# Two attention rows spread by TensorE, the stages around the first and last batch in another order, and elu added to x in two VectorE passes

## The reference, cut to what matters

```python
x: (8, 1024, 128) f32;  adj: (8, 1024, 1024) int32, 0 or 1, about 1 in 64 set
def gat(h, adj, W, a):                      # a graph attention layer
    Wh = h @ W
    e = (Wh @ a1)[:, :, None] + (Wh @ a2)[:, None, :]
    e = where(e > 0, e, 0.2 * e)            # leaky relu
    p = softmax(where(adj > 0, e, -big), axis=-1)
    return p @ Wh
x = x + elu(gat(relu(layernorm(x)), adj, W0, a0))     # layer 0
x = x + gat(relu(layernorm(x)), adj, W1, a1)          # layer 1
```

## Time and profile before

| what | value |
|---|---|
| median of 3 runs | 315.14 us (313.93 to 317.64) |
| the profiled execution, device time | 314.74 us |
| its span | 312.9 us |
| TensorE matmul busy | 293.6 us, 94% |
| VectorE busy | 267.3 us, 85% |
| ScalarE busy | 164.5 us, 53% |
| GpSimd busy | 47.6 us, 15% |
| granted TensorE clock over the span | 1.0 |
| chain that ended last: TensorE, VectorE, DMA, ScalarE | 74%, 10%, 4%, 4% |

### The profile page before, as it was taken

The page is one execution under the profiler, slowest core; times in us unless marked ns, Lnnn a source line. Parts: engine busy times, 40 slices in busy tenths (PEclk is TensorE's granted clock), DMA queues, the critical chain, the costliest instruction groups (busy, mean ns, idle before and its releaser), DMA issues.

```text
span 312.9 us, 6581 instructions
## 1 busy us (share of the span) xinstructions
PE 293.6 (94%) x2560; PEld 288.6 (92%) x2560; DVE 267.3 (85%) x610; ACT 164.5 (53%) x485; POOL 47.6 (15%) x53
## 2 busy tenths in 40 slices
PE   7999779799899999999999999999999999789695
PEld 7899679799899999999999999999999999788595
DVE  4596389949999989999899989999899959919785
ACT  3284480784493747483583648382674654353200
POOL 2612001220303030303003030303002000400000
PEclk9999999999999999999999999999999999999999
DMA  7997495102574334904574345713491302001211
GB/s 248 410 405 317 154 389 197 67 2 68 190 244 175 138 134 151 384 7 142 195 310 162 138 135 189 284 68 115 161 356 47 138 0 70 0 0 40 96 69 67
DMA packets 15247, 50.56 MB, mean 162 GB/s; under 512 B 2040, under 2 KB 3056, under 8 KB 15216
## 3 DMA queue, kind: packets, MB, share of 16 engines
q1 hardware_dynamic: 14640, 49.75, 43.0%
q10 hardware_dynamic: 576, 0.39, 0.4%
...
## 4 chain that ended last, share of the span: by engine, by line
PE 74%; DVE 10%; DMA 4%; ACT 4%; issue 4%; POOL 2%; POOLq 0%; DVEq 0%; ACTq 0%
PE acc L790 55%; PE prj L750 7%; PE tp L693 4%; DVE pbuf L564 4%; DMA row_r<-r_rows 3%; PE acc L806 2%; PE acc L690 2%; ACT xn L349 2%; POOL rstd L254 2%; DMA r_rows<-rT 1%; DVE stats L476 1%; DVE x_sb L594 1%; DVE ex L588 1%; PE prj L753 1%; DVE accs L573 1%
## 5 line engine op out<-in xcount | busy, mean ns | idle before, releaser
L790 PE MATMUL acc<-wh,pbuf 128*128 128x129 f32 x1984 | 232.9, 276 | 10.1 <-DVE accs L573 8.1
L790 PEld LDWEIGHTS acc<-wh,pbuf 128*128 128x128 f32 x1984 | 227.0, 192 | 13.3 <-issue 9.9
L564 DVE SCALAR_TENSOR_TENSOR pbuf<-row_r,sqr,adj_sb 128x1024 f32<-128x1024 f32 x127 | 157.8, 1278 | 8.8 <-DMA row_r<-r_rows 8.8
L254 POOL TENSOR_TENSOR rstd<-vareps,neg_half 128x8 f32<-128x8 f32 x15 | 37.5, 2503 | 213.9 <-DVE vareps L494 213.8
L379 ACT ACTIVATE accs<-accs,rec 128x128 f32<-128x128 f32 x120 | 36.7, 390 | 59.3 <-DVE rec L583 59.3
L349 ACT ACTIVATE xn<-x_sb,shift,rstd 128x128 f32<-128x128 f32 x120 | 47.6, 480 | 0.0
L368 ACT ACTIVATE wh<-prj,wh 128x128 f32<-128x128 f32 x120 | 31.6, 350 | 0.0
L750 PE MATMUL prj<-w_ext,hT 128*128 128x130 f32 x240 | 29.4, 275 | 0.1
L750 PEld LDWEIGHTS prj<-w_ext,hT 128*128 128x128 f32 x240 | 28.0, 191 | 0.2 <-ACT hT L355 0.2
L573 DVE TENSOR_TENSOR accs<-acc,uniform 128x387 f32<-128x387 f32 (+1 forms) x48 | 22.0, 508 | 4.2 <-PE acc L790 2.0
L476 DVE BATCH_NORM_STATS2 stats<-x_sb 128x6 f32<-128x128 f32 x120 | 24.6, 279 | 0.0
...
## 6 DMA issues: line engine op xcount, KB each, us to landing
...
r_rows<-rT SPq DMA_DIRECT2D x15, 4.0 KB
```

Source lines behind the costliest of these rows:

```text
L254: nc.gpsimd.tensor_tensor(rstd[:, :], vareps[:, :], neg_half[:, :], ALU.pow).then_inc(rstd_ready, 1)
L564: nc.vector.scalar_tensor_tensor(pbuf[:, t, :], row_r[:, n % 2, :], sqr[:, n % 2, 0, t:t + 1], adj_at(b, t), ALU.max, ALU.min).then_inc(p_ ...
L790: mm = nc.tensor.matmul(acc[:, k, s * C:(s + 1) * C], pbuf[:, t, i * P:(i + 1) * P], wh[:, n % 2, t, :], start=(t == 0 and s == 0), stop=( ...
```

## The change

Five things are changed together.

1. **Rows 1 and 15** (`SPREAD`) are made on the chip: `spread_r` (TensorE, 8 transposes in place of 1) and `copy_row` (ScalarE, two halves). SyncE no longer waits for row 1 before it issues adj of batch 2.
2. **elu** is written as max(h, 0) + min(exp(h), 1) - 1. `add_elu` adds max(hp, 0) straight to x, `add_x` adds min(ex, 1) to x, both as scalar_tensor_tensor on VectorE, and ScalarE's relu pass over ex is left out. The -1 is added by `add_hp` in layer 1 (the layer norm between them isn't changed by a constant). Batch 7 keeps the relu pass.
3. **The order of stages 0 to 4 and 12 to 15** is other on ScalarE, VectorE and TensorE. `before_drain(n)` says how many tiles are masked ahead of take_acc: 4 in stage 1, 1 in stage 3, 3 in stage 13, else 2.
4. **The head**: fewer dummy transposes; the two small products with a are apart, each with its weights' semaphore; the statistics of batch 1 are split around `copy_e_first`; the row's exp is taken ahead of the others.
5. **The end**: tile 7 of stage 15 is summed in a bank of `prj` that ScalarE fills beforehand with the uniform term (`seed_last`), and `last` has four parts, the fourth without a copy.

```diff
-    WARM = (24, 6, 4, 3)
+    WARM = (20, 2, 2, 3)
...
+        def before_drain(n):
+
+            return {1: 4, AHEAD: 1, LAST - 2: 3}.get(n, 2)
...
-            for m in range(1, AHEAD):
-                for t in range(T):
-                    load_adj(m, t)
-                load_x(m + 2)
-                load_row(m)
-
-                sp.wait_ge(row_in, 16 * m)
-            load_x(AHEAD + 2)
+            for t in range(T):
+                load_adj(1, t)
+            load_x(3)
+            for t in range(T):
+                load_adj(2, t)
+            load_row(2)
+            load_x(4)
+            load_x(5)
...
+            def copy_row(m):
+                k = spread_rows(m)
+                for h in range(2):
+                    act.wait_ge(row_spread, 2 * k + h + 1)
+                    cols = slice(h * (N // 2), (h + 1) * (N // 2))
+                    nc.scalar.activation(row_r[:, m % 2, cols], tp[:, cols],
+                                         ACT.Copy).then_inc(row_copied, 1)
...
                 act.wait_ge(hp_ready, e + 1)
                 if b > 0:
                     act.wait_ge(x1_ready, b)
                 nc.scalar.activation(ex[:, :, :], hp, ACT.Exp).then_inc(ex_ready, 1)
-                act.wait_ge(ex_ready, b + 1)
-                nc.scalar.activation(ex[:, :, :], ex[:, :, :], ACT.Relu, bias=1.0,
-                                     scale=-1.0).then_inc(elu_ready, 1)
+                if b == B - 1:
+                    act.wait_ge(ex_ready, B)
+                    nc.scalar.activation(ex[:, :, :], ex[:, :, :], ACT.Relu, bias=1.0,
+                                         scale=-1.0).then_inc(ex_ready, 1)
+
+            def seed_last():
+
+
+                act.wait_ge(wh_ready, T * LAST + T)
+                act.wait_ge(e_copied, 3 * LAST + 3)
+                nc.scalar.activation(LAST_TILE, uniform[:, LAST % 2, :],
+                                     ACT.Copy).then_inc(seeded_last, 1)
 
...
+            normalise(2)
+            exps(1)
...
+            copy_row(1)
...
                     copy_hT(n + 1)
+                scale_accs(n - 1)
+                if n + 1 in LATE or n + 2 in LATE:
                     elu_exp(n - 1) if elu else None
-                    normalise(n + 2) if n + 2 <= LAST else None
+                if n < LAST:
                     exps(n + 1)
-                    copy_r(n + 1)
-                elif n + 2 in LATE:
-                    elu_exp(n - 1)
-                    exps(n + 1)
-                    copy_r(n + 1)
-                elif n < LAST:
-                    exps(n + 1)
-                    copy_r(n + 1)
-                    elu_exp(n - 1) if elu else None
-                    normalise(n + 2) if n + 2 <= LAST else None
-                if n < LAST:
+                    if n + 1 in SPREAD:
+                        copy_row(n + 1)
+                    else:
+                        copy_r(n + 1)
+                    if n + 1 not in LATE and n + 2 not in LATE:
+                        elu_exp(n - 1) if elu else None
+                    if n + 2 <= LAST and n + 2 not in LATE:
+                        normalise(n + 2)
                     scale_wh(n + 1)
                 if n + 2 in LATE:
...
             def add_elu(b):
                 e = stage_of[0, b]
-                dve.wait_ge(elu_ready, b + 1)
-                nc.vector.scalar_tensor_tensor(ex[:, :, :], hp, 0.0, ex[:, :, :], ALU.max,
-                                               ALU.subtract).then_inc(hp_free, 1)
+                dve.wait_ge(hp_ready, e + 1)
+                nc.vector.scalar_tensor_tensor(x3_at(b), hp, 0.0, x3_at(b), ALU.max,
+                                               ALU.add).then_inc(x_half_added, 1)
 
             def add_x(b):
-                e = stage_of[0, b]
-                dve.wait_ge(hp_free, e + 1)
-                nc.vector.tensor_tensor(x3_at(b), x3_at(b), ex[:, :, :],
-                                        ALU.add).then_inc(x1_ready, 1)
+                dve.wait_ge(x_half_added, b + 1)
+                if b < B - 1:
+                    dve.wait_ge(ex_ready, b + 1)
+                    nc.vector.scalar_tensor_tensor(x3_at(b), ex[:, :, :], 1.0, x3_at(b), ALU.min,
+                                                   ALU.add).then_inc(x1_ready, 1)
+                else:
+                    dve.wait_ge(ex_ready, B + 1)
+                    nc.vector.scalar_tensor_tensor(x3_at(b), ex[:, :, :], -1.0, x3_at(b), ALU.mult,
+                                                   ALU.add).then_inc(x1_ready, 1)
 
             def add_hp(b):
                 e = stage_of[1, b]
                 dve.wait_ge(hp_ready, e + 1)
-                nc.vector.tensor_tensor(x3_at(b), hp, x3_at(b), ALU.add).then_inc(hp_free, 1)
+                nc.vector.scalar_tensor_tensor(x3_at(b), hp, -1.0, x3_at(b), ALU.add,
+                                               ALU.add).then_inc(x2_ready, 1)
 
...
+                for k, (lo, hi) in enumerate(last_parts):
+                    dve.wait_ge(acc_done, NB * LAST + k + 1)
+                    if k < NB:
+                        w = hi - lo
+                        nc.vector.tensor_tensor(
+                            accs[:, lo:hi, :],
+                            acc[:, k, 0:w * C].rearrange("p (s c) -> p s c", c=C),
+                            uniform[:, LAST % 2, :].unsqueeze(1).to_broadcast([P, w, C]),
+                            ALU.add).then_inc(acc_copied, 1)
+                        dve.wait_ge(acc_copied, NB * LAST + k + 1)
+                        sums, den = accs[:, lo:hi, 0:D], accs[:, lo:hi, D]
+                    else:
+                        sums, den = LAST_TILE[:, 0:D].unsqueeze(1), LAST_TILE[:, D:C]
+                    nc.vector.reciprocal(rec[:, lo:hi], den).then_inc(rec_ready, 1)
                     dve.wait_ge(rec_ready, LAST + k + 1)
...
-                if n + 2 <= LAST and n + 2 not in LATE and n + 1 not in LATE:
+                if n + 2 <= LAST and not {n, n + 1, n + 2} & set(LATE):
                     statistics(n + 2)
                     moments(n + 2)
-                masks(n, (0, 1))
+                masks(n, range(before_drain(n)))
                 take_acc(n - 1)
                 if n + 1 in LATE:
...
+                    copy_e(n + 1)
+                    masks(n, (5,))
+                    exp_args(n + 1)
+                elif n == 1:
                     copy_e(n + 1)
                     masks(n, (4,))
                     exp_args(n + 1)
                     masks(n, (5,))
+                    add_elu(b)
+                    add_x(b)
+                    masks(n, (6,))
+                    statistics(n + 2)
+                    moments(n + 2)
+                    masks(n, (7,))
+                    continue
+                elif n + 2 in LATE:
+                    masks(n, (3,))
+                    copy_e(n + 1)
+                    masks(n, (4,))
+                    exp_args(n + 1)
+                    masks(n, (5,))
+                    add_elu(b)
+                    add_x(b)
+                    statistics(n + 2)
+                    moments(n + 2)
+                    masks(n, (6, 7))
+                    continue
                 else:
+                    if before_drain(n) == 1:
...
-                        add_elu(b)
-                        masks(n, (4,))
-                        add_x(b)
-                        masks(n, (5, 6))
...
+            def spread_r(m):
+                pe.wait_ge(sqr_ready, m + 1)
+                for t in range(T):
+                    mm = nc.tensor.transpose(tp[:, t * P:(t + 1) * P],
+                                             sqr[:, m % 2, 2, t:t + 1].to_broadcast([P, P]),
+                                             ident[:, :])
+                    if t % 4 == 3:
+                        mm.then_inc(row_spread, 1)
...
-                                              start=(t == 0 and s == 0), stop=(t == T - 1),
-                                              skip_group_check=True)
+                        if t == 0 and n == LAST and i == T - 1:
+                            pe.wait_ge(seeded_last, 1)
+                        mm = nc.tensor.matmul(sum_of(n, i), pbuf[:, t, i * P:(i + 1) * P],
+                                              wh[:, n % 2, t, :], start=(t == 0 and s == 0),
+                                              stop=(t == T - 1), skip_group_check=True)
                         if t == T - 1 and s == tiles_in[k] - 1:
...
+                    if n < LAST and t == before_drain(n + 1) - 1:
                         mm.then_inc(p_used, 1)
...
-            for l in range(2):
-                mm = nc.tensor.matmul(prj[:, 0, 2 * l:2 * l + 2], w_tr[:, l, :], a_cols[:, l, :],
-                                      start=(l == 0), stop=True, skip_group_check=True)
-            mm.then_inc(wa_done, 1)
-            keep_warm(WARM[1])
...
             transposes(2)
             attend(0, (7,))
             for n in range(1, LAST):
```

(13 more changed lines are left out.)

189 lines of the change are left out of this document (122 added, 67 removed).

## The result

The changed kernel took **306.86 us** (median of 4 runs, 305.06 to 306.99) beside 314.53 us (4 runs, 313.68 to 317.64) of the kernel before: ratio 0.9725, 95% interval 0.968 to 0.9771. The profiled execution took 306.99 us, its span is 305.2; before it was 312.9. TensorE's matmuls are now busy for 292.0 us (96% of the span), and the chain that ended last lies on TensorE for 85% in place of 74%, on VectorE for 5% in place of 10%.

A forecast was written before the change was run, and what follows sets the result against it. TensorE alone was taken to bound the middle, with waits at both ends. The terms 2.2 + 4.6 - 1.8 + 3.9 - 0.1 = 8.8 us, off the median 315.14, gave 306.3 us, range 303.0 to 310.5.

The forecast's parts named there:

- The head and stage 0: Start to transposes(1): fewer dummies, split small products and an early row exp put transposes(1) at 19.45, not 19.80; 0.35 kept.
- The prediction's rule: GpSimd's power in the head: 2.61 us if it starts under a VectorE mask, 1.64 beside an idle VectorE.
- Row 1: Start of stage 1: the row made on the chip ends VectorE's wait; 2.2 us gained, the head's share included.
- Stages 1 and 2: Stage 1 to stage 3: 4.6 us gained, 37.25 against 41.9, with a new wait of 1.95 ahead of transposes(4).
- Stage 3: Stage 3 to stage 4: 1.8 us lost in waits for tile 3, xn of stage 5, sqr and the next sums.
- The middle: Stages 4 to 12: nothing gained, since TensorE bounds them and its work is left alone.
- Stages 13 to 15: Stage 13 to stage 15: stage 15 starts 6.2 us earlier; 3.9 kept once the wait for the seed is counted.
- The seed: First tile of stage 15: its eighth matmul waits 2.2 us (1.8 to 2.6) for seed_last, behind ScalarE's scaling.
- The tail: End of the kernel, last part's copy, reciprocals and products: 0.1 us lost, between 0.2 gained and 0.3 lost.
- that the waits don't come: Rival: xn of stage 4 and the seed are in time, 1.95 + 2.2 more gained, 302.1 us; chance 0.12.
- VectorE becomes the bound: Rival: stage 3's backlog stays or adj of batch 2 delays row 2; stages 2 to 5, 308.5 to 312; chance 0.15.
- The rival of the clock: Rival: the clock rises late, some 40 TensorE instructions of the head slower, 4.4 us at most, 308 to 310; chance 0.06.

The follow-up runs named there:

- the undone kernel: The changed kernel with row 1 through DRAM again and two masks, not four, ahead of the copied sums; 311.3 us, the second time 312.23 us.

## Why the prediction was right

The forecast, 306.3, is 0.6 below the median, inside its range, and the changed order did what the sum said. By its steps:

- **The head and stage 0** were sized too low and too high at once. transposes(1) began at 18.65, at the lower bound (18.6, no collision): the power took 1.67, the shift 0.20. The prediction's rule asks for an idle VectorE here; yet the power began at 13.17 under a half mask (13.05 to 13.80), one that reads its row factor from PSUM (the last section shows the lines). But the 0.4 us of small waits that was to go between there and stage 1 did not go: 18.65 to 36.71 is 18.06, the old 17.3 and the 0.77 of spread_r. Net 0.3 better than forecast, with the next point.
- **Row 1**: as forecast, the wait is gone; the undone kernel shows stage 1 at 39.32.
- **Stages 1 and 2**: 4.7 against 4.6. The new wait ahead of transposes(4) was priced at 1.95 and is 1.83. The wait ahead of stage 2, priced at 0.3 on an estimate from row 15, depends on the execution: nothing to see in the changed kernel's profile, 0.48 and 1.79 in others.
- **Stage 3** is the term that failed most: 2.98 lost against 1.8. The step was "xn of stage 5 comes 0.5 late, GpSimd's power being under a mask". The power did take the 2.61 it was given, and the statistics ended at 79.5 as worked out; but I took the old shift of 0.88 for granted, and under a longer run of passes it took 2.01. That makes 1.43 of the 0.5; the wait for tile 3 was 1.18 for 1.0. With the statistics moved to the front both waits were gone.
- **The middle**: nothing, exactly, and the relu pass kept for all batches moved nothing either.
- **Stages 13 to 15**: 6.75 against 6.2. Row 14 was in time, so the 0.45 left ahead of stage 14 did not appear. Row 15's share, undone alone, is 2.4.
- **The seed**: 1.86 against 2.2, in the place, with the releaser and for the reason given. What I put at nothing is what followed it: matmuls at a lower clock, 21.5 - 19.9 = 1.6 us between this profile's last stretch and that of the kernel with the old dummies, which has the same wait.
- **The tail**: from stage 15's start to the end that kernel needs 304.0 - 284.1 = 19.9 us, before it was 18.23; less the wait of 1.86 that is 0.2 gained, where 0.1 lost was written.
- **Some of the closeness is luck.** From stretch to stretch the errors are +0.3, +0.1, -1.2, +0.55 and -0.9: 7.7 kept in place of 8.8. Half of the 1.1 doesn't show in the median, because the kernel before came out at 314.53 where the forecast stood on 315.14. And the median holds the two variable times, of which the sum knew nothing; the fastest of the four runs took 305.06.

Of the rivals, that the waits don't come was wrong as posed: they came, and each could be taken out by moving one call, which gave 7 us more. "VectorE becomes the bound" was right in one particular, row 2 that lands late, and wrong in its cause: it was the write of 4 KB, at a time when the DMA engines were 4 or 5% busy, so adj of batch 2 was out of the way. The passes of the adds took 1.22. The rival of the clock looked at the head only; what the clock cost came in stage 15.
